# First tiles of a language-model tower: the gathers of a tile's embedding run ahead of the root of an earlier tile

## The reference

```python
def reference(x, token_table, op_table, var_table, const_table, struct_table, special_table, W_qkv, b_qkv,
              W_proj, b_proj, sim_matrix, gates, q_proj, k_proj, v_proj, o_proj):
    # x: 64 x 128 token numbers below 12500
    cat_table = concatenate([op_table, var_table, const_table, struct_table, special_table])   # 40 small rows, 12460 rows
    h = concatenate([token_table[x], cat_table[x]], axis=-1)          # 64 x 128 x 256, float32
    h = h + attn(layernorm(h))                                        # linear attention, phi = elu + 1, 16 heads of 16
    h = h + ffn(layernorm(h))                                         # gated experts: 16, the two best of each token,
    return h                                                          # causal softmax attention inside, head size 128
```

## Time and profile before

| | us |
|---|---|
| median of 3 runs | 1085.45 (1084.37 to 1086.52) |
| the profiled execution, its own time | 1086.31 |
| its span | 1084.6 |
| phase 1, first root to last | 25.4 to 391.6 |
| DVE busy | 873.4 (81%) |
| PE busy | 966.7 (89%) |
| POOL busy | 700.0 (65%) |

### The profile page before, as it was taken

The page is one execution under the profiler, slowest core; times in us unless marked ns, Lnnn a source line. Parts: engine busy times, 40 slices in busy tenths (PEclk is TensorE's granted clock), DMA queues, the critical chain, the costliest instruction groups (busy, mean ns, idle before and its releaser), DMA issues.

```text
span 1084.6 us, 23702 instructions
## 1 busy us (share of the span) xinstructions
PE 966.7 (89%) x6831; PEld 892.9 (82%) x6831; DVE 873.4 (81%) x2889; ACT 582.9 (54%) x1569; POOL 700.0 (65%) x924
## 2 busy tenths in 40 slices
PE   0788999999999835999999599999999999999998
PEld 0677887878788725899999499999999999999997
DVE  2568999999999865655555279999999999999998
ACT  1456666666666512544444255555555555555554
POOL 6667777777777678000000378888888888888885
PEclk9989999999999967999999789999999999999999
DMA  6465334444333236888888423333333333332331
GB/s 199 137 191 153 124 127 147 152 146 127 124 125 118 89 126 205 279 285 260 255 262 257 150 78 98 93 95 91 91 98 94 94 90 91 99 98 86 86 98 35
DMA packets 132325, 150.56 MB, mean 139 GB/s; under 512 B 14708, under 2 KB 119650, under 8 KB 132196
## 3 DMA queue, kind: packets, MB, share of 16 engines
q1 hardware_dynamic: 112964, 97.59, 29.0%
q0 software_dynamic: 18080, 50.36, 15.6%
q10 hardware_dynamic: 1152, 1.05, 0.3%
HBM read 83.79 MB, written 78.88 MB: 150 GB/s over the span
## 4 chain that ended last, share of the span: by engine, by line
DVE 39%; PE 38%; issue 9%; POOL 6%; DMA 6%; ACT 1%; SPq 0%; POOLq 0%; DVEq 0%; ACTq 0%
PE bank L1431 12%; PE bank L1433 10%; PE bank L1432 10%; DVE w_attn L1414 5%; DVE qk_e L1368 4%; DVE row_x L1408 3%; PE bank L1438 3%; DVE phi L1120 3%; DVE x L1368 3%; POOL sorted_x L745 2%; DVE attn L1132 2%; DVE kvm L1153 2%; DMA h<-in_L_tok_special_table,ids 2%; DVE stats L1160 2%; DMA row_x<-in_L_tok_special_table,ids 2%
## 5 line engine op out<-in xcount | busy, mean ns | idle before, releaser
L1431 PE MATMUL bank<-wo_hi,split_lo 128*128 128x256 f32 x1024 | 304.6, 297 | 10.1 <-DVE x L1368 4.6
L1433 PE MATMUL bank<-wo_hi,split_hi 128*128 128x256 f32 x1024 | 288.8, 282 | 0.0
L1432 PE MATMUL bank<-wo_lo,split_hi 128*128 128x256 f32 x1024 | 288.5, 282 | 0.0
L1431 PEld LDWEIGHTS bank<-wo_hi,split_lo 128*128 128x128 f32 x1024 | 194.0, 189 | 23.6 <-DVE qk_e L1368 11.6
L1432 PEld LDWEIGHTS bank<-wo_lo,split_hi 128*128 128x128 f32 x1024 | 194.1, 190 | 0.0
L1433 PEld LDWEIGHTS bank<-wo_hi,split_hi 128*128 128x128 f32 x1024 | 193.6, 189 | 0.0
L940 ACT ACTIVATE h<-bank,rwo 128x256 f32<-128x256 f32 x256 | 107.5, 471 | 115.6 <-PE bank L1433 111.6
L818 POOL DMA_INDIRECT row_y<-sorted_y,pair_now x128 | 124.5, 972 | 31.2 <-issue 21.3
L811 POOL COPY pair_now<-pair_at 128x2 uint32<-128x2 uint32 x64 | 11.9, 186 | 178.0 <-SPq L599 178.0
L1269 DVE TENSOR_TENSOR split_lo<-bank,split_hi 128x256 fp32r<-128x256 f32 x144 | 60.8, 423 | 69.3 <-ACT split_hi L902 67.9
L1368 DVE SCALAR_TENSOR_TENSOR x<-bank,rwo,x 128x256 f32<-128x256 f32 x256 | 108.5, 473 | 2.7 <-PE bank L1433 1.9
(11 more groups left out here) (228 smaller groups left out, 2664.7 us busy)
## 6 DMA issues: line engine op xcount, KB each, us to landing
sorted_y<-row_y SPq DMA_DIRECT2D x36, 384.0 KB, 3.1
sorted_y<-w_attn SPq DMA_DIRECT2D x36, 384.0 KB, 3.1
row_x<-sorted_x SPq DMA_DIRECT2D x72, 128.0 KB, 2.9
h_rows<-h SPq DMA_DIRECT2D x64, 128.0 KB, 1.7
row_x<-h_rows SPq DMA_DIRECT2D x64, 128.0 KB, 2.2
out_h<-row_x SPq DMA_DIRECT2D x64, 128.0 KB, 1.7
embed_table<-in_L_tok_token_table SPq DMA_DIRECT2D x10, 625.0 KB
embed_table<-in_L_tok_special_table SPq DMA_DIRECT2D x10, 623.0 KB
```

The costliest lines, as they stand in the source:

```text
L1431: pe.matmul(ps, left[1][c], right[0][c], start=(c == 0), stop=False)
L1432: pe.matmul(ps, left[0][c], right[1][c], start=False, stop=False)
L1433: last = pe.matmul(ps, left[0][c], right[0][c], start=False, stop=(c == n - 1))
```

## The change

- POOL no longer waits for `small_loaded` at the start, but ahead of sm0 only.
- POOL's step of the first 14 tiles becomes: root, tk, sm, and then sp of the next tile. Small is issued a step earlier than before, and so is special, against the root of its step.
- The roots of rows 0 and 1 are formed in steps -6 and -5, behind small; those of rows 2 and 3 in steps -3 and -2, ahead of token; from step 0 on, row i.c + 4 as before. No root is formed in steps -4 and -1.
- sim_inv moves from step -5 to the end of step -1, and DVE's `simn` from step -4 to step 0.
- DVE's `w_attn_s[1]` moves from the head of step -5 to its end, and stats(1) from the end of step -5 to step -4, behind centers(0).
- SP's list is the same: the table copies stand where they stood.

POOL's list is then: sp0 tk0 sm0 sp1, tk1 sm1 root0 sp2, tk2 sm2 root1 sp3, tk3 sm3 sp4, root2 tk4 sm4 sp5, root3 tk5 sm5 sp6, tk6 sm6 sp7 sim_inv, root4 tk7 sm7 sp8, and so on to root10 tk13 sm13, then root11 and the joined gather of tile 14.

```diff
--- before.py
+++ after.py
@@ -685,7 +685,6 @@
 
             pool.wait_ge(consts_ready, N_CONSTS)
             pool.wait_ge(setup_v, 2)
-            pool.wait_ge(small_loaded, 64)
 
             waits_taken = [0]
 
@@ -702,36 +701,55 @@
             def offsets(index):
                 return bass.IndirectOffsetOnAxis(ap=index, axis=0)
 
-            def step1(i):
-                if i.j is None and i.c == -5:
-                    pool.wait_ge(setup_v, 4)
-                    pool.tensor_tensor(sim_inv[:, :], sim_norm[:, :], minus_half[:, :], ALU.pow
-                                       ).then_inc(setup_p, 1)
-                gather, small_rows = i.shift(7), i.shift(6)
-
-                row = i.c + 4
+            def special_rows(tile):
+                if in_parts(tile):
+                    pool.indirect_dma_start(out=h[tile.c % 8][:, HALF:C], out_offset=None, in_=special_table,
+                                            in_offset=offsets(ids[:, tile.c, 1:2]),
+                                            bounds_check=N_SPECIAL - 1, oob_is_err=False
+                                            ).then_inc(special_gathered[tile.q], 16)
+
+            def token_rows(tile):
+                if in_parts(tile):
+                    pool.indirect_dma_start(out=h[tile.c % 8][:, 0:HALF], out_offset=None, in_=token_table,
+                                            in_offset=offsets(ids[:, tile.c, 0:1])
+                                            ).then_inc(rows_gathered[tile.q], 16)
+
+            def small_rows(tile):
+                if in_parts(tile):
+                    if tile.c == 0:
+                        pool.wait_ge(small_loaded, 64)
+
+                    landed_quarter(pool, special_gathered, tile)
+                    pool.indirect_dma_start(out=h[tile.c % 8][:, HALF:C], out_offset=None,
+                                            in_=category,
+                                            in_offset=offsets(ids[:, tile.c, 0:1]),
+                                            bounds_check=N_SMALL - 1, oob_is_err=False
+                                            ).then_inc(rows_gathered[tile.q], 16)
+
+            def form_roots(row):
                 if 0 <= row < N_ROOTS:
                     pool.wait_ge(done["roots_in"], row + 1)
                     pool.tensor_tensor(roots[:, row, :], roots_in[:, row, :], minus_half[:, 0:3], ALU.pow
                                        ).then_inc(done["roots"], 1)
-                if in_parts(small_rows):
-
-                    landed_quarter(pool, special_gathered, small_rows)
-                    pool.indirect_dma_start(out=h[small_rows.c % 8][:, HALF:C], out_offset=None,
-                                            in_=category,
-                                            in_offset=offsets(ids[:, small_rows.c, 0:1]),
-                                            bounds_check=N_SMALL - 1, oob_is_err=False
-                                            ).then_inc(rows_gathered[small_rows.q], 16)
-                if in_parts(gather):
-
-                    pool.indirect_dma_start(out=h[gather.c % 8][:, HALF:C], out_offset=None, in_=special_table,
-                                            in_offset=offsets(ids[:, gather.c, 1:2]),
-                                            bounds_check=N_SPECIAL - 1, oob_is_err=False
-                                            ).then_inc(special_gathered[gather.q], 16)
-                    pool.indirect_dma_start(out=h[gather.c % 8][:, 0:HALF], out_offset=None, in_=token_table,
-                                            in_offset=offsets(ids[:, gather.c, 0:1])
-                                            ).then_inc(rows_gathered[gather.q], 16)
-                elif gather.inside(B):
+
+            def step1(i):
+                gather = i.shift(7)
+                if i.c == -7:
+                    special_rows(gather)
+                if i.c in (-3, -2):
+                    form_roots(i.c + 5)
+                elif i.c >= 0:
+                    form_roots(i.c + 4)
+                token_rows(gather)
+                small_rows(gather)
+                if i.c in (-6, -5):
+                    form_roots(i.c + 6)
+                special_rows(gather.shift(1))
+                if i.c == -1:
+                    pool.wait_ge(setup_v, 4)
+                    pool.tensor_tensor(sim_inv[:, :], sim_norm[:, :], minus_half[:, :], ALU.pow
+                                       ).then_inc(setup_p, 1)
+                if gather.inside(B) and not in_parts(gather):
                     if gather.c == JOINED_FROM:
                         pool.wait_ge(rows_joined, 16 * (2 * COPIES + 4))
                     pool.indirect_dma_start(out=h[gather.c % 8], out_offset=None, in_=embed,
@@ -1094,12 +1112,12 @@
                 gate_wait("position")
                 dve.tensor_copy(position_u[:, tiles, :], pair_in_x[:, tiles, :]).then_inc(done["position_index"], 1)
 
+            def row_stats(tile, slot):
+                rows_landed(dve, tile.c)
+                dve.bn_stats(stats[:, 2 * slot, :], h[tile.c % 8]).then_inc(done["ln1_stats"], 1)
+
             def step1(i):
-                if i.c == -5:
-                    dve.wait_ge(setup_a, 4)
-                    dve.tensor_tensor(w_attn_s[1], w_attn[:, :, :], w_attn_s[0].bitcast(F32), ALU.subtract
-                                      ).then_inc(setup_v, 1)
-                if i.c == -4:
+                if i.c == 0:
                     dve.wait_ge(setup_p, 1)
                     dve.scalar_tensor_tensor(simn[:, :, :], sim[:, :, :], float(C) ** -0.5,
                                              sim_inv[:, :].unsqueeze(1).broadcast_to([P, CH, E]), ALU.mult, ALU.mult
@@ -1111,6 +1129,8 @@
                     dve.wait_ge(done["roots"], row + 1)
                     dve.scalar_tensor_tensor(centers[:, row, :], moments[:, row, :, 0], -1.0, roots[:, row, 0:2],
                                              ALU.mult, ALU.mult).then_inc(done["centers"], 1)
+                if i.c == -4:
+                    row_stats(Tile(1), 0)
                 for n in weights_at(i.c - 1):
                     weight_lo(dve, n)
                 if phi_tile.inside(B):
@@ -1172,10 +1192,12 @@
                     g = group_at(i.c - back)
                     if g is not None:
                         piece(g)
-                if stats_tile.inside(B):
-
-                    rows_landed(dve, stats_tile.c)
-                    dve.bn_stats(stats[:, 2 * (1 - i.p), :], h[stats_tile.c % 8]).then_inc(done["ln1_stats"], 1)
+                if i.c == -5:
+                    dve.wait_ge(setup_a, 4)
+                    dve.tensor_tensor(w_attn_s[1], w_attn[:, :, :], w_attn_s[0].bitcast(F32), ALU.subtract
+                                      ).then_inc(setup_v, 1)
+                if stats_tile.inside(B) and i.c != -5:
+                    row_stats(stats_tile, 1 - i.p)
 
             run1(dve, step1)
 
```

## The result

The changed kernel takes 1093.47 us, the median of 4 runs (1092.12 to 1094.80), against 1085.99 for the kernel before on the same chip (4 runs). The ratio is 1.007, with a 95% interval of 1.0052 to 1.0089. The profiled execution took 1093.11 us, 6.8 us more than that of before.

What follows compares the result with a forecast made beforehand. No engine bounds the whole span; in the touched stage (49 to 100 us) DVE has slack and waits. Root4's +8.0 and the later steps' -0.7 give 7.3 us on 1086.31, 1093.6; less 0.86 for the median, 1092.7 us, range 1086 to 1098.

Steps and rivals of the forecast that it cites:

- rival A: The forecast itself: root4 held by sp6's landing and sim_inv, the lead repaying little; 1089.5 to 1098 us, chance 0.62.
- The start: Up to root3: centers(0) some 3 us sooner, 0.7 us of the head start left by root3 (bounds 0 and 3).
- root4: Two tiles' gathers, sp6's landing and sim_inv ahead of root4 delay centers(4) by 8.0 us (bounds 4.8 and 8.0).
- simn: DVE's simn, moved to step 0: costs nothing, 0.2 us behind sim_inv and already ready before root4.
- From root4 to root12: Eight steps from centers(4) to centers(12): 42.4 + 1.3 + 2.4 + 2.7 = 48.8 us against 49.53, so -0.7 (bounds -7.1 and +6.9).
- the clock: After the gap at root4: PE idles, the granted TensorE clock falls to 0.50, costing 1.3 us (bounds 0 and 2).
- the ring of gathers: POOL's steps between root4 and root12: 1.5 special gathers meet table copies at 1.8 us each, 2.7 us (bounds 0 and 9).
- the joined gather: Ahead of root12: the gather waits for short copies issued behind h2(8), so +2.4 us stays (bounds 0 and 3).
- The lead itself: From root4 on, small issued ahead of the root gives its landing about a step of slack; stats waits of tiles 8 and 12 go.
- Rival C: Faster: special lands within POOL's own work each step and the lead removes every landing wait; -3.0 us, 1082.4; chance 0.06.
- Rival B: root4 held only by POOL's work (+4.8), lead repays part: 1087 to 1089.5 (0.13), or within 2.2 us (0.11).
- rival D: The ring locks onto the copies, each special gather meeting them: +8 + 5 us or more, 1098 to 1101; chance 0.05.

Runs made afterwards that it cites:

- e4: Changed kernel without the 24 table copies, gathering only the token half of rows from tile 14 on: 1077.46 us.
- e5: Kernel before without the 24 table copies, gathering only the token half of rows from tile 14 on: 1075.25 us.
- e2: Changed kernel with roots of rows 2 to 11 a step sooner in POOL's list, sim_inv left late: 1094.42 us.
- e3: Changed kernel with roots of rows 2 to 11 a step sooner and sim_inv back between tk1 and sm1: 1086.46 us.
- changed, again: The changed kernel, unaltered, measured a second time beside other runs on the same chip: 1095.03 us.
- e1: Changed kernel with sim_inv alone back between tk1 and sm1: 1092.29 us, and 1092.90 us when run again.
- e10: Kernel before with only sim_inv moved to the end of step -1 and simn to step 0: 1087.49 us.
- e6: Changed kernel with roots of rows 2 to 11 a step sooner, sim_inv between tk1 and sm1, and first table copies held back for stats(0) to stats(4): 1091.28 us.
- e7: Kernel before with only the first table copies held back for stats(0) to stats(4): 1088.05 us.

## Why the prediction was right

The forecast was 1092.7 us, from rival A's mechanism, and the measurement 1093.47; the wait ahead of root4 was forecast to make up all of the loss, and does. That the two numbers lie within 1 us of each other is partly luck, as the terms show, and the same kernel's second series gave 1095.03. Term by term:

**The start.** Forecast: 3 us sooner at centers(0), 0.7 of it left at root3. Measured: 3.95, and root3 at 43.06 against 43.50, 0.44. The reason given, that stats(1) and sm2 wait for landings as before, fits the pair e4 and e5, where the landings are short and the start, with sim_inv out of it, is worth 5.9 us. The prediction's word that sim_inv's leaving frees nothing holds with the copies only: sm1 waits 3.92 us for sp1 in the changed kernel, and 1.12 in e4.

**root4.** Forecast +8.0 at centers(4), bounds 4.8 and 8.0; measured 7.2. sp6 landed in 4.15 us instead of the 4.99 taken from the earlier trace rows; root3 came 0.26 us later than forecast, and nothing else differs by more than 0.1. From root3 to root4 there are 8.37 us more than before: sim_inv is 2.93 of them, sm6's wait 2.33 (2.63 less the usual 0.30), and the rest, 3.11, is the second tile's three gathers (3.90) less the 0.79 us that POOL stood idle ahead of root4 before. The lower bound was mistaken: it let sm6 follow tk6 at once, which no landing seen here allows (e4). The estimate by the Trainium skill (DMA: Bandwidth & Descriptors, "Anatomy of one DMA — SWDGE (gpsimd) path"), 2.15 us for such a DMA, is below the shortest landing of special in these traces, 2.5 us. With the 0.78 us behind it even 2.15 would have made sm6 wait 0.35 us, so the prediction was wrong to call the landing hidden by that figure.

**simn.** Forecast: costs nothing, since sim_inv is ready before root4. It is ready before root4 and adds nothing to the sum, but the statement passed over a second guard: simn waits 6.08 us for sim_inv, ahead of centers(4), and with it alone (e2) the loss is the same. What I called one chain of POOL's work behind one wait is two waits that end 0.8 us apart.

**From root4 to root12.** Forecast 48.8 us, measured 48.78 (57.82 to 106.60). The sum is right and its terms are not, so that it fits is luck; the second trace of the same kernel has 50.5. Against steps of 5.30 the two behind the gap are 0.8 us too long together (forecast 1.3, the clock). The granted clock of 0.50 lasts until 62, inside the first of them, which has 0.6 of it; that the clock is the cause is not shown. The four from centers(7) to centers(11) are 4.8 too long (2.7, the ring of gathers); POOL waited for special in each. The last, with the joined gather, is 0.8 too long (2.4). I had it begin from a root11 on time; sm13's wait of 3.19 us made root11 late, and the short copies were on their way meanwhile.

**The lead itself.** It removes the stats waits, as forecast. It wins nothing: eight steps take 48.8 us with it, 49.5 in the kernel before and 48.4 in e3, which has no lead either. Other traces gave 50.5 (changed, again), 51.6 (e1) and 50.6 (e1, again) with it, 50.4 (e2) and 48.7 (e10) without: the two kinds overlap, and nothing speaks for a gain. Rival C, the lead repaying more than the wait, needed landings within POOL's own work. From tile 7 on e4 has them, small waits for none there, and still the lead doesn't pay (43.5 us against 43.0 in e5).

Rival B's 4.8 us at root4 and rival D's eight gathers in the copies' way both didn't happen. Left open: why sp6's landing in e1 was longer in both traces (4.15 and 4.35 us in the changed kernel, 5.02 and 5.07 in e1). In all four sp6 is issued 0.56 to 0.57 us ahead of the same table copy, so its place beside that copy doesn't tell them apart; it may be chance. Open as well is how much of e1's remaining delay is sp6's landing and how much the second tile's gathers, since no kernel takes away one alone.

## What to carry to other kernels

A lead in a software pipeline isn't free in the step in which it is built: here one step got two tiles' gathers, a landing and a `pow` of 2.9 us ahead of a root that all engines wait for, and that one gap (7.2 us, of which 6.45 are left at centers(12)) is the whole loss. Look for every guard of a late instruction before undoing one: two waits that end at nearly the same time hide each other, and only the kernel with both edits showed their price. A latency is worth hiding only where it is the last wait; where a serial list of gathers sets the pace, an earlier place for its consumer's rows only moves the wait from DVE to POOL.

## What the runs showed of the hardware that I had not expected

Copies from HBM to HBM on SP's queue, about 624 KB each, lengthen the landing of a small gather issued by POOL from a median of 2.5 to 2.7 us (e5 and e4) to one of 4.0 to 4.1 in the same two orders (2.8 to 4.6 in the other kernels with copies). No other placing of them beat the first: held back in the start they cost 2.9 us more in the order before and 4.8 in e3's, and with two of them moved into a quiet stretch nothing and 1.7. In the order before they cost 10.65 us altogether (1085.90 against 1075.25 in e5's series), and centers(12) moves by 10.05. Where three of them were issued right ahead of a 128 KB store (e6), the issue of that store took 4.36 us instead of 0.33, and it landed after 8.35 us, where the median of these stores is 1.7; in e7 the issues of two such stores took 2.99 us.
